# A two-layer graph attention kernel: how the second layer gets its turned membership matrices

## What is computed

```python
# layer 0: transformer attention over edges, then projection, norms, feed-forward
score = einsum('ehd,ehd->eh', K[src], Q[dst]) / sqrt(32) + edge_bias
m = segment_max(score, dst); ex = exp(score - m[dst])
out = segment_sum(ex / segment_sum(ex, dst)[dst] * V[src], dst)
# layer 1: graph attention on feat = (h @ W_lin + b) @ W_gat
e = leaky_relu(el[src] + er[dst], 0.2)          # 8 numbers for an edge
m = segment_max(e, dst); e = exp(e - m[dst])
out = segment_sum(e / segment_sum(e, dst)[dst] * feat[src], dst)
```

## Time and profile before

| | us |
|---|---|
| median of 3 runs (7329.08 to 7333.42) | 7331.24 |
| the profiled execution | 7368.06 |
| its span, first to last instruction | 7366.1 |

### The profile page before, as it was taken

How to read it: one execution, slowest core, us unless ns; L and a number is a source line. 1 busy time by engine, 2 the same in 40 slices (tenths; PEclk the granted TensorE clock), 3 DMA queues, 4 the chain that set the end, 5 groups by cost and what they waited for, 6 DMA issues and landing times. The chain is left out here.

```text
span 7366.1 us, 117463 instructions
## 1 busy us (share of the span) xinstructions
PE 5928.6 (80%) x25898; PEld 4640.5 (63%) x25898; DVE 4984.4 (68%) x12562; ACT 3060.9 (42%) x10078; POOL 3669.2 (50%) x4022
## 2 busy tenths in 40 slices
PE   8967777777777777777999976788888788887888
PEld 5545555555555555556999965666666666666666
DVE  4567777777777777776777754666665656655677
ACT  3344444444444444443333333444444444444440
POOL 1154555445545544452444455555555555555543
PEclk9988888888988898888999986666666666666679
DMA  5577777777777777774222235666666566665659
GB/s 182 198 208 219 222 219 224 209 214 223 218 211 216 225 219 214 218 220 121 83 86 83 85 97 144 165 163 163 169 165 163 161 163 163 164 163 161 164 150 294
DMA packets 722949, 1312.97 MB, mean 178 GB/s; under 512 B 109087, under 2 KB 502131, under 8 KB 722420
## 3 DMA queue, kind: packets, MB, share of 16 engines
q0 software_dynamic: 200192, 634.41, 32.3%
q1 hardware_dynamic: 416578, 396.48, 18.6%
q10 hardware_dynamic: 105650, 276.43, 10.1%
HBM read 964.16 MB, written 342.73 MB: 177 GB/s over the span
## 5 line engine op out<-in xcount | busy, mean ns | idle before, releaser
L817 PE MATMUL bank<-ev,oh 128*128 128x264 f32 x7040 | 2565.5, 500 | 55.3 <-DVE ev L1289 44.0
L515 POOL DMA_INDIRECT Gf<-kv_tab,srcs x1564 | 1502.3, 961 | 1496.8 <-DVE ev L1289 1000.3
L515 POOL DMA_INDIRECT Gf<-ft_tab,srcs x1564 | 1588.0, 1015 | 1173.9 <-DVE ev L1289 746.2
L817 PEld LDWEIGHTS bank<-ev,oh 128*128 128x128 f32 x7040 | 1634.3, 246 | 354.5 <-DVE ev L1289 68.0
L1289 DVE TENSOR_TENSOR ev<-Gf,ex 128x528 f32<-128x528 f32 x1760 | 1232.3, 700 | 2.1 <-ACT ex L679 1.3
L817 PE MATMUL bank<-qs,oht 128*128 128x256 f32 x3520 | 1039.6, 422 | 223.2 <-issue 116.6
L817 PE MATMUL bank<-Gf 128*128 128x128 f32 (+3 forms) x6284 | 1195.3, 343 | 4.4 <-ACT Gf L572 3.2
L611 ACT ACTIVATE absd<-lane,dlocs 128x128 f32<-128x128 f32 x3520 | 1112.6, 389 | 3.7 <-DVE bms L1164 3.7
L817 PEld LDWEIGHTS bank<-Gf 128*128 128x128 f32 x6284 | 935.7, 191 | 171.3 <-issue 98.4
L817 PEld LDWEIGHTS bank<-qs,oht 128*128 128x128 f32 x3520 | 666.0, 210 | 425.7 <-issue 352.9
L1304 DVE SCALAR_TENSOR_TENSOR acc<-acc,same,bank 128x264 f32<-128x264 f32 x1540 | 737.2, 479 | 192.5 <-remote 115.1
(11 more groups left out here) (158 smaller groups left out, 6806.3 us busy)
## 6 DMA issues: line engine op xcount, KB each, us to landing
sums<-acc ACTq DMA_DIRECT2D x440, 528.0 KB
qs<-q_tab SPq DMA_DIRECT2D x880, 128.0 KB
qs<-dst_tab SPq DMA_DIRECT2D x880, 128.0 KB
Gf<-sums SPq DMA_DIRECT2D x196, 132.0 KB, 2.6
kv_tab<-Gf SPq DMA_DIRECT2D x98, 260.0 KB, 2.1
Gf<-in_x SPq DMA_DIRECT2D x196, 128.0 KB, 2.2
Gf<-kv_tab,srcs POOLq DMA_INDIRECT x1564
Gf<-ft_tab,srcs POOLq DMA_INDIRECT x1564
```

The costliest lines, as they stand in the source:

```text
L515: pool.indirect_dma_start(out=rows[layer][:, m % SLOTS[layer], k, :], out_offset=None, in_=tab, in_offset=bass.IndirectOffsetOnAxis(ap=src ...
L817: return nc.tensor.matmul(o, a, r, start=first, stop=end)
```

## The change

The second layer now gets `oht` as the first does. PE's `turns` and ACT's `turned` run in both layers (440 groups of four in all instead of 220 in the first alone), and `spread` takes its weights from `oht[:, (s // 2) % 2, ...]`. The 880 loads by SP, the table `dst_tab` with its one store, the registers for the spans, and the 880 comparisons on DVE are gone. The one-hot itself (`oh`), the gathers and everything behind the scores stay as they are.

```diff
-        dst_tab = dram("dst_tab", ((LC * P + 1) * SPAN,))
-        ohs = [v[:, k * SPAN:(k + 1) * SPAN] for v in (oht[...], prod[...]) for k in range(4)]
-            sp.wait_ge(S_["rec_f"], LC)
-            sp.dma_start(dst_tab[SPAN:].rearrange("(c p n) -> p c n", c=LC, p=P),
-                         rec[:, :, 0:SPAN]).then_inc(S_["rec_ld"], 16)
-            def dst_rows(B, s, n):
-                p, r = step_at(B, s - ST)
-                if p.live:
-                    sp.wait_ge(E_["oht_cp"], ohs_made(p, r))
-                sp.dma_start(qs[:, s, :], dst_tab[bass.ds(n * SPAN, SPAN)].partition_broadcast(P)).then_inc(qld[s], 16)
-            for u in range(NS):
-                if u % ST == 0:
-                    at = span_rows(u // ST)
-                dst_rows(Blk(u // ST, 1), u % ST, at[u % ST])
             def first_node(B):
-                act.wait_ge(E_["oht_cp"], ohs_made(B, 0) if B.layer else B.c * 4 + 1)
+                act.wait_ge(E_["oht_cp"], B.c * 4 + 1)
                             C, r = step_at(B, s + 4)
-                            if C.live and layer == 0:
+                            if C.live:
                                 turned(C, r // 2)
             def spread(layer, B, s):
-                if layer == 1:
-                    pe.wait_ge(E_["oht_cp"], ohs_made(B, s))
-                elif s % 2 == 0:
+                if s % 2 == 0:
                     pe.wait_ge(E_["oht_cp"], B.c * 4 + s // 2 + 1)
-                        m = mm(bank[2 + s % 2][:, k * H:(k + 1) * H], ohs[s][:, k * P:(k + 1) * P], erq[:, s, :])
+                        m = mm(bank[2 + s % 2][:, k * H:(k + 1) * H], oht[:, (s // 2) % 2, 2 * (s % 2) + k, :], erq[:, s, :])
-                        if s % 2 == 0 and layer == 0:
+                        if s % 2 == 0:
                             C, r = step_at(B, s + 4)
                             if C.live:
                                 turns(C, r // 2)
-            def members(B, s):
-                dve.wait_ge(qld[s], 16 * (NB + B.n + 1))
-                p, r = step_at(B, s - ST)
-                if p.live:
-                    dve.wait_ge(E_["qexp"], p.c * ST + r + 1)
-                    if s == 0:
-                        dve.wait_ge(E_["oh0_made"], 2 * p.c + 2)
-                V.tensor_scalar(ohs[s], qs[:, s, :], tile_of[:, B.n * ST + s:B.n * ST + s + 1], None,
-                                ALU.is_equal).then_inc(E_["oht_cp"], 1)
-                        C, r = step_at(B, s + 6)
-                        if layer == 1 and C.live:
-                            members(C, r)
```

More of the change, by code:

```diff
@@ L267, in build @@
         fin_a, fin_b, fin_p, fin_o, fin_d = [[carve(w) for _ in range(3)] for w in (D, D, D, D, 2 * H)]
-        ohs = [v[:, k * SPAN:(k + 1) * SPAN] for v in (oht[:, :, :, :].rearrange("p a k n -> p (a k n)"),
-                                                       prod[:, :, :, :].rearrange("p a k n -> p (a k n)")) for k in range(4)]
         dloc, lk, bm = [v[:, :, :].rearrange("p (b s) k -> p b (s k)", s=ST) for v in (dlocs, lks, bms)]
@@ L301, in gathered @@
             return 32 * (m // (2 * ST) + 1 + layer * len(range(m % (2 * ST), NSPAN, 2 * ST)))
-        def ohs_made(B, s):
-            return 4 * NB + B.n * ST + s + 1
         def onehot(B, s):
@@ L526, in _ @@
             pool.wait_ge(S_["m_w"], 16)
-            pool.wait_ge(S_["rec_ld"], 16 * (LC + 1))
+            pool.wait_ge(S_["rec_ld"], 16 * LC)
             pool.wait_ge(S_["tables"], 8)
@@ L751, in edge_phase @@
                     onehots(z, g)
-                for g in range(2 if layer == 0 else 0):
+                for g in range(2):
                     turned(z, g)
@@ L1351, in edge_phase @@
                 landed[0] = landings(layer, 0)
-                if layer == 1:
-                    for s in range(6):
-                        members(Blk(0, 1), s)
                 for b in range(NB + 2):
```

## The result

| kernel | median us | lowest to highest | runs |
|---|---|---|---|
| before | 7340.93 | 7322.76 to 7500.51 | 13 |
| changed | 7379.79 | 7341.51 to 7406.87 | 13 |

The changed kernel takes 1.0054 times as long, 95% interval 1.0039 to 1.007: 39 us more, where 30 less were forecast. The one execution of 7500.51 us is a slow one and is left out of the ratio. The profiled execution of the changed kernel, 7341.51 us, was its lowest run, and the profiled one of the kernel before (7368.06) lay above its median. So the two spans must not be subtracted; waits, periods and clocks of the second phase can be compared.

A forecast was written before the change was run, and what follows sets the result against it. The second edge phase was taken as bound by POOL's round of gather issues and waits; -0.35 - 0.82 + 0.9 = -0.27 us a block, x 110 = -30 us, gave 7300 us, main case 7180 to 7390, whole range 7030 to 7470.

The forecast's parts named there:

- comparisons and gathers: Second edge phase: one comparison gone before POOL's restart, -0.35 us a block, and shorter gather issues on POOL, -0.82.
- the copies on ACT: Four copies a block in the second phase, 2.4 us of ACT, taken at nothing because needed two or more steps later.
- The turns on PE: Group of transposes at s = 2 ahead of `maxima_turned` delays POOL's second wait: +0.9 us a block, bounds 0 and +0.9.
- The round of POOL: Second phase: a block's period is POOL's restart, gather issues, one more wait and landing: 25.4 us for 25.24 measured.
- the 2.5 named: Sign: a block with 16 gathers should take about 2.5 us longer than one with 14 if the period follows POOL.
- the 0.35 us before the restart: DVE's comparison between the scan and the `weigh` that restarts POOL goes: -0.35 us a block, bounds -0.35 and 0.
- the bound of 2.1 us: If the copies' cover fails, PE waits for a one-hot as in the first layer: 2.1 us a block.
- The sum: Second phase: -0.35 - 0.82 + 0.9 = -0.27 us a block, x 110 = -30 us.
- PE as the bound: Rival, second phase: turns make PE the bound, +1.3 to +2.3 us a block, about 7520 us; chance 0.24.
- The stall at the scan: Rival: less DMA traffic ends DVE's scan wait, -4.8 us a block, 6800 us, half of it 7065; chance 0.16.
- The clock rose and nothing followed: Rival: PE granted 0.75 or more, worth 0.35 us a block or 40 us; inside the main case of 0.6.
- What would show it: Second-phase signs: period 25.0 us, gathers 0.96, POOL's waits 4.4 and about 2.7, scan 1.7 to 2.0 behind POOL's last issue.

The follow-up runs named there:

- one-hots first: Changed kernel with layer 2's one-hots made on ACT ahead of the copy and one step earlier: 5902.68 us, 0.9946 of the kernel before on the same chip.
- the removal: Changed kernel without layer 2's turns and copies, so only loads and comparisons go: 7321.44 us (0.9962 of before); again on another chip 7207.35 us (0.9931).
- Turns alone: Changed kernel without ACT's copies and PE's wait for them in layer 2, turns kept: 7230.84 us (0.9945 of before), again 7215.29 us (0.9937).
- the odd version: Changed kernel with layer 2's turns and copies one step later, at odd s: 7227.60 us (0.9941 of before), again 7227.30 us (0.9933).
- narrow gathers: Changed kernel with layer 2's gathers 8 numbers wide instead of 272, as many issued: 7413.45 us, one run.

## Why the prediction failed

Two steps failed. The first is the term on which the direction hung: comparisons and gathers were to give 1.17 us a block, and gave 0.23 on the chip 7347 and 0.52 on 7265. The second is the copies on ACT, put at nothing, which cost 0.36 us a block on 7265. The turns on PE, put at +0.9, cost 0.07 there, some 0.2 more at most; that they were priced too high took back part of the two errors, by luck.

*The round of POOL.* Right in outline: a block with 16 gathers takes 2.0 us longer than one with 14 in the kernel before and 2.2 in the changed one (averages 25.2 and 27.2, 25.2 and 27.4 us), near the 2.5 named. (These are the gathers issued between two scans, so a block that is long for another cause counts more of them too; the sign that the prediction named is met, but it is a weak one.) The chip 5934 shows the bare round, 18.6 us for 18.5 of issues. What failed is the inference that each 0.1 us taken from the round comes off the period. By the two periods, 25.2 and 18.6, some 6.6 us of the round are waits that a chip without late completions does not have (it may differ in more, and the second period is that of one-hots first), and they shift when work is moved: the 0.35 us before the restart brought 0.16, the full way to the maximum moved from 7.6 to 8.5 us for 0.07, both on chips with late completions.

*Comparisons and gathers, -1.17 us.* **This is the step that failed in size, and it carried the forecast's direction.** It measured -0.23 us a block on the chip 7347 and -0.52 on 7265. Its cause failed in the main part too: the gathers went from 1.018 to 0.99 us, not to the 0.960 of the first layer, and on the chip 5934, with no comparison in the kernel, they still last 1.003. Only 0.03 of the 0.058 us goes with comparisons or loads, which no run parts; the rest of the difference between the layers has another reason, which stays open.

*Turns on PE, +0.9 us.* The delay was real (7.6 to 8.5 us), its price was 0.07 us by the medians and 0.15 by the phase, near the lower bound named. That the forecast came no further out is luck: this cost was set too high while the next one was left out.

*Copies on ACT, taken at nothing.* **This is the cover that failed.** The text argued that the copy waits for PE's turn, and that what stands behind it on ACT is needed two or more steps later. It did not ask how long that wait is, though completions are late in nearly every block of this phase (92 of 101 at the scan), and it left out that PE's own next turns and `row_values`'s copy stand behind it. The cost, +0.36 us a block, lies well inside the bound of 2.1 us that was given for the failing cover; the value taken should not have been its end at zero. In the first layer the same copy had such a wait (207.5 us), and the earlier trace rows show what PE waits for behind it. Moved to odd s, turns and copies together cost nothing that can be told from the removal (7227.3 and 7207.4 us), so the price lay in their place and not in their work.

*The sum.* On the chip 7265 the parts are -0.52, +0.07 and +0.36, together -0.09 us a block, -10 us. On the chip 7347 the removal is -0.23 (7347.18 to 7321.44); turns and copies together are +0.40 with loads and comparisons beside them (7390.83). As an estimate without them, the result's ratio put on that chip gives 7347.18 x 1.0054 = 7386.9 for the changed kernel, and so +0.59. The forecast set 1.17 gained against 0.9 lost. Where the change loses, the gain was five times too large and the cost one and a half times; the sign hung on the first. How the cost there splits between turns and copies was not measured.

*The rivals.* PE as the bound did not come: the period rose by 0.17 us and not by 1.3, and PE's busy time fell. The stall at the scan did go in part, from 583.6 to 167.3 us, but not to the gain of that rival, for it reappeared at three other places. That it can go whole, with all POOL's gathers left, the chip 5934 shows: 25.4 - 18.6 = 6.8 us a block against the 4.8 that the rival had named, but not by anything the change does. The clock rose and nothing followed: that rival was right as far as it went.

*The clock.* Turns alone, beside the removal on the same chip, granted 0.75 instead of 0.67 in 4500 to 7050 us, at 7215 and 7207 us:

```profile
4500.00:7050.00 2550.00, 2072.08 (x7825) 1607.49 (x7825) 1385.54 (x3739) 1136.26 (x4262) 1439.30 (x1451) 0.67 0.42 127
```
```profile
4500.00:7050.00 2550.00, 2071.54 (x9435) 1665.05 (x9435) 1376.60 (x3712) 1133.22 (x4246) 1420.19 (x1444) 0.75 0.42 126
```

The higher granted clock, with the turns that came with it, bought nothing that can be measured, and it is 0.91 where nothing stalls. The Trainium skill (TensorE: Matmul & The Clock Gate, Part 4: PE-mode transpose) says that transposes don't count as activity for the clock; 1600 more transposes in this window went with a higher clock at the same busy time of PE (2071.54 and 2072.08 us), so the trace does not agree with it here. The rival of 7520 us, which it would have put first, did not come.

*What would show it.* The period was 25.41, not 25.0; gathers 0.998, not 0.96; POOL's first wait 3.29 us in the block shown, its second 3.78 (forecast 4.4 and 2.7), and a third came. The scan started 2.4 us behind POOL's last issue there, but no longer waiting for PE itself: `el_er` had, and `weigh` stood between. The signs named would have told that the sum was wrong.

## What stays open

Why PE's completions are late on four chips (or five; the first two may be one) and not on another isn't known. The runs show only that halving the number of gathers ends it, and that cutting the traffic to little over a third does not. Why the changed kernel loses 0.54% on one chip and gains 0.17% on another is open too. Turns and copies cost 0.9% on the one and 0.5% on the other, and the removal gives 0.4% and 0.7%; a chip on which completions are later would charge more for each new wait on PE, but that is argued and not shown. And it stays open whether the copies cost what they do through the one-hots behind them or through the way to the maximum: the run that was to tell met the chip where nothing is late.

## What to carry to other kernels

When a trace is full of waits for completions that arrive long after the instruction's recorded end, price every new wait on that engine, and what is queued behind it, before the work itself: here 16 transposes in a block cost 0.07 us, which can't be told from nothing, and the four copies that wait for them 0.36. Look at a wait's kind before its engine; a stall that ends "remote" moves when work is moved. Neither its disappearance at one line nor the sum over all lines tells the gain: on the chip 7265 the odd version has 1044.4 us of such waits and the changed kernel 886.9, and the odd version is 28 us faster. And never set variants measured on one chip against the original measured on another: more than half of a gain of 1.1% was the chip.

## What the runs showed of the hardware

- Chips differ by 19% on the same program: 7341 us and 5934 us for the kernel before. On the fast one its granted clock over the whole span was 0.894 to 0.906, against 0.807 in the profiled one. In the two kernels profiled there, no completion of PE was late in the windows of either edge phase.
- DVE and ACT waited 928 us of 2550 for late completions at four places while POOL issued indirect gathers, single ones almost 5 us behind PE's recorded (modelled) end (5442.58 to 5447.40). With half as many gathers it was 13 us of 1780; with little over a third of the bytes (46 instead of 122 GB/s) it stayed, at 942 us.
- 115 MB of broadcast loads and 880 comparisons changed the ratio by nothing measurable beside turns and copies (1.0052 with them on the chip 7347, 1.0054 without on 7341), while without turns and copies their removal gave 0.4% (7347) and 0.7% (7265).
- A gather issue of POOL took 0.989 us in the mean with rows of 8 numbers and 0.998 with rows of 272 (narrow gathers and the changed kernel).
